# Three PSUM banks in one ring for the maxima products and the projections of the masked attention layers

## The chip, the cores and the metric

The kernel runs on one core of a Trainium2 chip. A time is the device time of one execution in microseconds (us). The parts of a core are called PE (TensorE, the matmul engine, with PEld for its weight loads), DVE (VectorE), ACT (ScalarE), POOL (GpSimd) and SP (SyncE, which here only issues DMAs). PE writes its results to PSUM, a memory of eight banks of 128 x 512 fp32 values; DVE and ACT read them from there. The engines run independently and meet at semaphores.

## The reference, cut to what matters

The network has four layers of attention and feed-forward over `x` of shape (8, 512, 256). Layers 0, 1 and 3 have attention under a mask; layer 2 (relative positions) and the four feed-forward parts are not touched by the change.

```python
# layer 1 (layers 0 and 3 alike, without adj and with a finite value for masked scores)
Q, K, V = heads(layernorm(x), Wq), heads(ctx, Wk), heads(ctx, Wv)   # 16 heads of 16
scores  = einsum('bhqd,bhkd->bhqk', Q, K) / sqrt(16) + adj
scores  = where(mask == 0, -inf, scores)
out     = einsum('bhqk,bhkd->bhqd', softmax(scores, axis=-1), V)
x       = x + out.transpose(0, 2, 1, 3).reshape(b, s, 256) @ Wo.T + bo
```

## The kernel before, in words

`masked_attention` does one masked layer. A layer is a row of frames, one for each of the 8 batches (b from -1, which only prepares, to 8, which only finishes). A frame has 16 steps s and each step two positions, p = 2s and p = 2s + 1; every engine walks through the same 32 positions in an order written out by hand, and they differ only in what they wait for.

The row maxima come first, in a product of their own, seven steps ahead of their use. In position p PE makes two of them, which this text calls p1(2p) and p1(2p+1) (line 261, one 96-row bf16 matmul of 128 x 512 each). DVE adds the mask and takes the maximum (line 460), and the semaphore `maxed` says that it has read the bank. The two banks `p1_ps0` and `p1_ps1` alternate, so p1(u) waits until p1(u-2) has been read.

In the same position PE makes the scores of two heads, transposed, into `p2_ps` (line 276). In even positions ACT has put the mask there before (the "seed", line 512); in odd positions of layers 0 and 3 PE adds it with two more matmuls (line 281). In layer 1 ACT seeds both. ACT takes the exponential (line 529). At the end of each odd position PE multiplies the probabilities of the step before by V (line 292, eight instructions).

Between these stand the shared units, which all use the one bank `front_ps`: the transposes of the normalized input (xT, line 223), the projections k, q (line 230), v (line 235) and out (line 242), and the turned maxima m (line 251). A unit of the first five kinds has two pieces. In PE's order of an even position it is: p1(2p), scores, piece 0, p1(2p+1), piece 1. The units stand at positions 0 (v0), 4 (v1), 8 (out0), 12 (out1), 14 and 16 (xT0, xT1), 20 and 22 (k0, k1), 24 and 28 (q0, q1); m stands at 3, 11, 19 and 27, behind the scores of an odd position, and also waits for `m_split`, the last of four small DVE instructions (line 414) that stand between and behind the maxima of the position before. A unit of position p is read in position p + 1: xT, k, q and m by ACT, which in position p + 1 comes to it before that position's exponential but behind the exponential and the seed of position p; v and out by DVE, before the maxima of position p + 1. The semaphore `front_read` counts these reads, and each unit waits for the one before it.

A layer starts with eight units in a row, `FIRST` (xT0, xT1, k0, k1, q0, q1, v0, v1), all through `front_ps`. DVE splits the two k and the two q results into three bf16 parts each (lines 430 to 436), SP stacks them by twelve DMAs (line 613) into `k_stack` and `q_stack`, and the first p1 waits for both stacks. SP gives out these DMAs behind loads of masks, which wait for POOL. At the end of a layer out0 and out1 follow each other.

## Time and profile before

| | us |
|---|---|
| median of 3 runs | 3845.13 (3836.37 to 3846.18) |
| the profiled execution | 3849.17 |
| its span, first to last instruction | 3847.4 |
| PE busy | 3198.5 (83%) |
| DVE busy | 2500.1 (65%) |
| ACT busy | 2215.1 (58%) |
| POOL busy | 1118.4 (29%) |
| p1 matmuls (line 261), 1536 of them | 603.0, idle before them 119.2 |
| maxima (line 460), 1536 of them | 1038.7, idle before them 434.5 |
| exponentials (line 529), 768 of them | 781.3, idle before them 275.4 |

The masked layers run from 16 to 671 us (layer 0), from 975 to 1702 us (layer 1) and from 2782 to 3437 us (layer 3). Shares over the whole span mix them with the other stages, so a masked layer has to be read from its own stretch. "Idle before" is time in which the engine did nothing ahead of an instruction of the group; the name behind the arrow is what it waited for. A matmul's time in the trace reaches from its start to the end of its result, and consecutive matmuls overlap, so the distance between two starts says more than the duration: two p1 next to each other start 0.22 us apart if nothing holds them. A row of busy time by stretch (rows 1) gives the stretch, its length, then for PE, PEld, DVE, ACT and POOL the busy time and the number of instructions, then the granted clock of TensorE as a share of 2.4 GHz, the busy share of the DMA engines and GB/s.

### The profile page before, as it was taken

The numbers are of one execution on the slowest core, as the hardware profiler recorded it, in microseconds if no ns is written. First come the engines' busy times: TensorE is split into PE (matmuls) and PEld (weight loads), VectorE is DVE, ScalarE is ACT, GpSimd is POOL, SyncE is SP. The second block draws the span as 40 slices with busy tenths as digits, with TensorE's granted clock in tenths as the row PEclk, the third lists the DMA queues.
The fourth block names the chain that finished last, engine by engine and source line by source line (L and its number), as shares of the span: only waits on it lengthen the run. The fifth ranks groups of instructions, "written<-read, shape, count | busy, mean of one in ns | idle before, by whom it ended". The sixth has DMA issues, their size and how long they took to land. (4 is left out here: it accounts for less than half of the span.)

```text
span 3847.4 us, 67593 instructions
## 1 busy us (share of the span) xinstructions
PE 3198.5 (83%) x17361; PEld 1628.5 (42%) x17361; DVE 2500.1 (65%) x7668; ACT 2215.1 (58%) x2970; POOL 1118.4 (29%) x1194
## 2 busy tenths in 40 slices
PE   5999998899588888858987888888379999965997
PEld 3343332344333333225654555555134334325565
DVE  4777775777677677744225777878867777755431
ACT  1777777444188888962115666667537777750111
POOL 4344440000545555401104333321232211101332
PEclk8999999899799899988998999999589999985899
DMA  5322420000433333310018998997031221102232
GB/s 146 87 70 73 101 62 12 22 1 1 130 105 89 89 94 89 83 52 0 0 39 277 293 292 288 308 310 267 19 87 40 56 63 40 35 25 97 74 101 66
DMA packets 212153, 392.86 MB, mean 102 GB/s; under 512 B 24633, under 2 KB 76985, under 8 KB 211657
## 3 DMA queue, kind: packets, MB, share of 16 engines
q1 hardware_dynamic: 168777, 296.38, 27.8%
q10 hardware_dynamic: 36864, 83.90, 5.8%
q0 software_dynamic: 6144, 8.39, 1.3%
q8 instruction: 143, 2.34, 0.3%
q14 instruction: 225, 1.84, 0.2%
HBM read 189.88 MB, written 96.47 MB: 74 GB/s over the span
## 5 line engine op out<-in xcount | busy, mean ns | idle before, releaser
L460 DVE CUSTOM_DVE_ANT_0 A_sums<-A_p_ps,A_bias 128x512 bf16<-128x512 f32 x1536 | 1038.7, 687 | 434.5 <-PE A_p_ps L261 397.1
L529 ACT ACTIVATE A_probs<-A_p_ps 128x1024 f32<-128x1024 f32 x768 | 781.3, 1018 | 275.4 <-PE A_p_ps L276 184.9
L261 PE MATMUL A_p_ps<-A_k_stack,A_q_stack 96*128 96x512 bf16 x1536 | 603.0, 395 | 119.2 <-DVE A_nmax L460 110.3
L512 ACT ACTIVATE A_p_ps<-A_biasT 128x1024 f32<-128x1024 bf16 (+1 forms) x512 | 526.1, 1028 | 62.3 <-ACT A_probs L529 2.8
L276 PE MATMUL A_p_ps<-A_q_stack,A_k_stack 99*128 99x512 bf16 x1536 | 468.1, 386 | 41.3 <-ACT A_p_ps L512 36.6
L292 PE MATMUL A_oT_ps<-A_probs,A_v_aug 128*17 128x512 f32 x3072 | 417.5, 616 | 0.7 <-ACT A_probs L529 0.7
L261 PEld LDWEIGHTS A_p_ps<-A_k_stack,A_q_stack 96*128 96x128 bf16 x1536 | 149.4, 97 | 634.3 <-DVE A_nmax L460 541.5
L1100 DVE CUSTOM_DVE_ANT_0 A_scores<-A_qk_ps,A_rel_in 128x384 f32<-128x384 f32 (+3 forms) x512 | 232.4, 486 | 83.2 <-PE A_qk_ps L984 75.3
L1007 PE MATMUL A_t_ps<-ident,A_scores 128*128 128x128 f32 x1280 | 228.8, 301 | 58.2 <-DVE A_probsT L1090 49.9
L1090 DVE COPY A_probsT<-A_t_ps 128x384 f32<-128x384 f32 (+3 forms) x512 | 229.4, 485 | 55.7 <-PE A_t_ps L1007 48.2
L1155 ACT ACTIVATE A_rel_out<-A_rel_ps 128x1024 f32<-128x1024 f32 (+3 forms) x256 | 180.2, 704 | 144.8 <-PE A_rel_ps L973 143.5
L1162 ACT ACTIVATE A_scores<-A_scores,A_nmax 128x384 f32<-128x384 f32 (+3 forms) x512 | 257.5, 555 | 7.6 <-DVE A_nmax L1100 7.4
L276 PEld LDWEIGHTS A_p_ps<-A_q_stack,A_k_stack 99*128 99x128 bf16 x1536 | 143.4, 99 | 179.4 <-ACT A_p_ps L512 73.2
L1182 POOL TENSOR_SCALAR_AFFINE_SELECT A_rel_in<-A_rel_in 128x256 f32<-128x256 f32 x256 | 103.4, 412 | 396.3 <-DMA A_rel_in<-A_rel_dram 390.5
L1007 PEld LDWEIGHTS A_t_ps<-ident,A_scores 128*128 128x128 f32 x1280 | 152.3, 149 | 135.5 <-DVE A_probsT L1090 57.0
L574 POOL TENSOR_SCALAR A_bias<-A_mask_in 128x512 bf16<-128x512 int32 (+2 forms) x68 | 132.0, 1941 | 207.6 <-DVE A_nmax L460 187.5
L1517 PE MATMUL B_cv_ps<-B_hs,B_tap_diag 128*128 128x512 f32 x384 | 180.6, 607 | 2.6 <-DVE B_hs L1619 2.4
L574 POOL TENSOR_SCALAR A_biasT<-A_mask_in 128x512 bf16<-128x512 int32 (+2 forms) x68 | 131.8, 1938 | 138.8 <-PE A_p_ps L281 70.2
L2773 ACT ACTIVATE M_hid<-M_h_ps,M_b 128x512 f32<-128x512 f32 x64 | 44.0, 688 | 189.3 <-PE M_h_ps L2575 185.7
L281 PE MATMUL A_p_ps<-A_biasT,ident_bf 128*128 128x512 bf16 x512 | 152.5, 378 | 0.0
L555 POOL CAST A_parts<-A_qk 128x512 bf16<-128x512 f32 x84 | 51.3, 611 | 336.1 <-ACT A_qk L497 335.6
L2092 ACT ACTIVATE U_hid<-U_h_ps,U_hid_bias 128x512 f32<-128x512 f32 x64 | 44.0, 687 | 177.5 <-PE U_h_ps L1930 177.5
(343 smaller groups left out, 5436.4 us busy)
## 6 DMA issues: line engine op xcount, KB each, us to landing
A_k_stack<-A_parts SPq DMA_DIRECT2D x192, 256.0 KB, 5.0
A_q_stack<-A_parts SPq DMA_DIRECT2D x192, 256.0 KB, 5.5
A_rel_dram<-A_rel_out ACTq DMA_DIRECT2D x64, 512.0 KB, 4.9
A_rel_in<-A_rel_dram SPq DMA_DIRECT2D x64, 512.0 KB, 5.3
A_rel_dram<-A_rel_out ACTq DMA_DIRECT2D x64, 384.0 KB, 4.8
A_rel_in<-A_rel_dram SPq DMA_DIRECT2D x64, 384.0 KB, 5.1
A_ctxT<-in_ctxT SPq DMA_DIRECT2D x32, 512.0 KB, 6.5
A_mask_in<-in_mask SPq DMA_DIRECT2D x64, 256.0 KB, 4.7
```

Source lines behind the costliest of these rows:

```text
L261: nc.tensor.matmul(p1_ps[i % 2][:, :], q_stack[0:KS, a_par, j * GH + i, t * P:(t + 1) * P], k_stack[0:KS, a_par, j * GH + i, :], start=Tru ...
L276: last = nc.tensor.matmul(p2_ps[half][:, i % 2, :], k_stack[:, par, j * GH + i, kb * P:(kb + 1) * P], q_stack[:, par, j * GH + i, :], star ...
L292: nc.tensor.matmul(oT_ps[CW * i:CW * i + HD + 1, :], v_aug[:, v_par, kb, j * GH + i, :], probs[:, (s - 1) % 2 * 2 + i // 2, i % 2, :], sta ...
L460: nc.vector.tensor_tensor_reduce(out=sums[:, i % NX, :], in0=p1_ps[i % 2][:, :], in1=bias[:, t, :], scale=-1.0, scalar=3.4028235e38, op0=A ...
L512: nc.scalar.activation(p2_ps[half][:, :, :], turned, ACT.Copy).then_inc(seeded, 1)
L529: nc.scalar.activation(probs[:, s % 2 * 2 + half, :, :], p2_ps[half][:, :, :], ACT.Exp).then_inc(exp_done, 1)
L574: last = nc.gpsimd.tensor_scalar(dst, mask_in[:, k % 2, :], 0.0, NEG, ALU.is_equal, ALU.mult)
L1007: last = nc.tensor.transpose(t_ps[:, i, kb, :], scores[(p - TURN_LAG) % NP][:, i, kb * P:(kb + 1) * P], ident[:, :])
L1090: nc.vector.tensor_copy(probsT[u % NP][:, i, 0:nk, :], t_ps[:, i, 0:nk, :]).then_inc(copied, 1)
L1100: nc.vector.tensor_tensor_reduce(out=scores[p % NP][:, i, 0:n], in0=qk_ps[i][:, 0:n], in1=rel_in[s % NI][:, (2 * half + i) * n:(2 * half + ...
L1162: nc.scalar.activation(scores[u % NP][:, i, 0:n], scores[u % NP][:, i, 0:n], ACT.Exp, bias=nmax[:, u % NP, i:i + 1], scale=-1.0).then_inc( ...
L1517: last = nc.tensor.matmul(cv_ps[c % 2][:, :], tap_diag[:, c, k, :], hs[:, c % 2, k:k + S], start=k == 0, stop=k == 2)
```

## The change

`p1_ps0`, `p1_ps1` and `front_ps` become `ring_ps0` to `ring_ps2`. The turns of a frame are listed in PE's order, `p1(2p)`, the shared unit of position p if there is one, `p1(2p+1)`; each takes the next of the three banks. There are 78 turns in a frame, 26 times three, so a turn has the same bank in every frame. A turn waits until the turn three before it has been read. `front_read` is split into `act_read` and `dve_read`, as two engines' counts can no longer be one count. The number and the order of the instructions on PE, DVE, ACT, POOL and SP stay; what changes is which semaphore and value a turn waits for, and which bank it uses.

```diff
-        p1_ps = [pb(f"p1_ps{i}", [P, S], F32) for i in range(2)]
+        ring_ps = [pb(f"ring_ps{i}", [P, S], F32) for i in range(RING)]
...
-        front_ps = pb("front_ps", [P, S], F32)
...
-        front_read = sem("front_read")
+        act_read, dve_read = sem("act_read"), sem("dve_read")
...
+        def ring_turns():
+
+            turns = []
+            for p in range(HALVES):
+                turns.append(("p1", 2 * p))
+                turns += [(k, i) for _, k, i in shared(PLAN, p)]
+                turns.append(("p1", 2 * p + 1))
+            return turns
...
+        def wait_for_bank(pe, b, kind, i):
+
+            at = TURNS.index((kind, i))
+            same = [u for n, u in enumerate(TURNS) if n % RING == at % RING]
+            here = same.index((kind, i))
+            for back, turns in ((0, same[:here]), (1, same)):
+                for k, n in reversed(turns):
+                    if in_ring(b - back, k, n):
+                        if k == "p1":
+                            pe.wait_ge(maxed, ((b - back) * STEPS + LEAD) * GH + n + 1)
+                        else:
+                            pe.wait_ge(dve_read if k in ("v", "out") else act_read, read_of(b - back, k, n))
+                        return
...
         def pe_max_unit(pe, b, a, a_par, i):
-            unit = (b * STEPS + a) * GH + i
             _, _, j, t = ahead(a - LEAD)
-            if later(unit - 1):
-                pe.wait_ge(maxed, unit - 1)
-            nc.tensor.matmul(p1_ps[i % 2][:, :], q_stack[0:KS, a_par, j * GH + i, t * P:(t + 1) * P],
+            turn = ("p1", (a - LEAD) * GH + i)
+            wait_for_bank(pe, b, *turn)
+            nc.tensor.matmul(bank(*turn)[:, :], q_stack[0:KS, a_par, j * GH + i, t * P:(t + 1) * P],
                              k_stack[0:KS, a_par, j * GH + i, :], start=True, stop=True).then_inc(p1_done, 1)
...
-                for n, kind, i in here:
-                    pe_shared(pe, n, kind, i, uses_before(b), b, 0)
                 for n, kind, i in shared(plan, p):
                     if kind == "m":
-                        pe_maxima(pe, n, i, uses_before(b), b)
+                        pe_maxima(pe, i, b)
+                    else:
+                        wait_for_bank(pe, b, kind, i)
+                        pe_shared(pe, bank(kind, i), kind, i, b, 0)
...
+                if n >= RING:
+                    pe.wait_ge(dve_read if FIRST[n - RING][0] == "v" else act_read, first_read(n - RING))
                 for piece in range(2):
-                    pe_shared(pe, n, kind, i, 0, -2, piece)
+                    pe_shared(pe, ring_ps[n % RING], kind, i, -2, piece)
```

On PE, in positions 14 and 15 of a steady frame of layer 0 (xT0 and the position behind it; `A0_qk32` is the normalized input, `ISA` an instruction that computes a wait's value or waits), before the change:

```order
L223 MATMUL A0_front_ps<-ident,A0_qk32 128x128
L260 ISA
L261 MATMUL A0_p1_ps1<-A0_k_stack,A0_q_stack 128x512 [waits A0_maxed]
L223 MATMUL A0_front_ps<-ident,A0_qk32 128x128 x2
L260 ISA
L261 MATMUL A0_p1_ps0<-A0_k_stack,A0_q_stack 128x512 [waits A0_maxed]
L274 ISA
L276 MATMUL A0_p2_ps1<-A0_q_stack,A0_k_stack 128x512 [waits A0_exp_done]
L276 MATMUL A0_p2_ps1<-A0_q_stack,A0_k_stack 128x512
L281 MATMUL A0_p2_ps1<-A0_biasT,ident_bf 128x512 x2
L260 ISA
L261 MATMUL A0_p1_ps1<-A0_k_stack,A0_q_stack 128x512 [waits A0_maxed]
```

and with the change, in the same place:

```order
L282 MATMUL A0_ring_ps2<-ident,A0_qk32 128x128
L237 ISA
L322 MATMUL A0_ring_ps0<-A0_k_stack,A0_q_stack 128x512 [waits A0_maxed]
L282 MATMUL A0_ring_ps2<-ident,A0_qk32 128x128 x2
L237 ISA
L322 MATMUL A0_ring_ps1<-A0_k_stack,A0_q_stack 128x512 [waits A0_maxed]
L335 ISA
L337 MATMUL A0_p2_ps1<-A0_q_stack,A0_k_stack 128x512 [waits A0_exp_done]
L337 MATMUL A0_p2_ps1<-A0_q_stack,A0_k_stack 128x512
L342 MATMUL A0_p2_ps1<-A0_biasT,ident_bf 128x512 x2
L239 ISA
L322 MATMUL A0_ring_ps2<-A0_k_stack,A0_q_stack 128x512 [waits A0_act_read]
```

Nothing moved, but the last of these, p1(31), now uses the bank of xT0 and waits for ACT's read of it, where it waited for a maximum before. The same holds at the second p1 behind every shared unit of an even position; behind v and out the wait is for `dve_read`.

On PE, in the first shared units of layer 0, before and with the change:

```order
L223 MATMUL A0_front_ps<-ident,A0_qk32 128x128 [waits A0_xn_ready]
L223 MATMUL A0_front_ps<-ident,A0_qk32 128x128 x3
L223 MATMUL A0_front_ps<-ident,A0_qk32 128x128 [waits A0_front_read]
L223 MATMUL A0_front_ps<-ident,A0_qk32 128x128 x3
L230 MATMUL A0_front_ps<-A0_ctxT,A0_wk 128x256 [waits built,A0_front_read,zeroed]
L230 MATMUL A0_front_ps<-A0_ctxT,A0_wk 128x256 x3
L230 MATMUL A0_front_ps<-A0_ctxT,A0_wk 128x256 [waits A0_front_read]
L230 MATMUL A0_front_ps<-A0_ctxT,A0_wk 128x256 x3
```

```order
L282 MATMUL A0_ring_ps0<-ident,A0_qk32 128x128 [waits A0_xn_ready]
L282 MATMUL A0_ring_ps0<-ident,A0_qk32 128x128 x3
L282 MATMUL A0_ring_ps1<-ident,A0_qk32 128x128 x4
L291 MATMUL A0_ring_ps2<-A0_ctxT,A0_wk 128x256 [waits built,zeroed]
L291 MATMUL A0_ring_ps2<-A0_ctxT,A0_wk 128x256 x3
L291 MATMUL A0_ring_ps0<-A0_ctxT,A0_wk 128x256 [waits A0_act_read]
L291 MATMUL A0_ring_ps0<-A0_ctxT,A0_wk 128x256 x3
```

xT1 no longer waits for the read of xT0, and likewise k0 and k1 run up to three units ahead of their reads.

## Rows read from the trace of the kernel before

**Rows 1.** Busy time by stretch: steady part of layer 0, of layer 1.

```profile
170.00:640.00 470.00, 441.03 (x2367) 179.97 (x2364) 363.90 (x1115) 357.00 (x393) 181.10 (x143) 1.00 0.28 70
1080.00:1640.00 560.00, 471.15 (x2311) 182.87 (x2309) 406.25 (x1218) 487.64 (x533) 282.65 (x224) 0.93 0.33 91
```

**Rows 2.** Groups by line: the p1 matmuls, busy, mean ns, idle before.

```profile
L261 PE MATMUL A_p_ps<-A_k_stack,A_q_stack 96*128 96x512 bf16 x1536 | 603.0, 395 | 119.2 <-DVE A_nmax L460 110.3 <-issue 4.9 <-DMA A_q_stack<-A_parts 1.8
```

**Rows 3.** Timeline (start, us, instruction), layer 0: end of maximum 12, p1(14).

```profile
324.66 0.08 DVE L460 DVE_READ_ACCUMULATOR2_ANT A_nmax<- 128x1 f32 x1
...
324.80 0.39 PE L261 MATMUL A_p_ps<-A_k_stack,A_q_stack 96*128 96x512 bf16 x1 [0.30 <-DVE A_nmax L460]
```

**Rows 4.** Timeline, layer 0: p1(31), the read of xT0, scores of position 16.

```profile
345.37 0.38 PE L261 MATMUL A_p_ps<-A_k_stack,A_q_stack 96*128 96x512 bf16 x1
...
345.99 0.58 ACT L484 ACTIVATE A_xnT<-A_front_ps 128x512 f32<-128x512 f32 x1
...
346.89 0.60 PE L276 MATMUL A_p_ps<-A_q_stack,A_k_stack 99*128 99x512 bf16 x2
```

**Rows 5.** Timeline, layer 0, the read of k0 and p1(43).

```profile
357.86 0.67 ACT L497 ACTIVATE A_qk<-A_front_ps,A_bk 128x512 f32<-128x512 f32 x1
...
358.50 0.38 PE L261 MATMUL A_p_ps<-A_k_stack,A_q_stack 96*128 96x512 bf16 x1
```

**Rows 6.** Timeline, layer 0: reads of v1 and out1, with p1(11) and p1(27).

```profile
321.81 0.72 DVE L374 TENSOR_TENSOR A_v_aug<-A_front_ps,A_bv_bc 128x256 f32<-128x256 f32 x2
322.17 0.38 PE L261 MATMUL A_p_ps<-A_k_stack,A_q_stack 96*128 96x512 bf16 x1
...
341.29 0.65 DVE L394 TENSOR_TENSOR x_sb<-A_front_ps,x_sb 128x512 f32 x1
341.64 0.38 PE L261 MATMUL A_p_ps<-A_k_stack,A_q_stack 96*128 96x512 bf16 x1
```

**Rows 7.** Timeline, layer 0: p1(38), the last split, m.

```profile
351.99 0.39 PE L261 MATMUL A_p_ps<-A_k_stack,A_q_stack 96*128 96x512 bf16 x1 [0.56 <-DVE A_nmax L460]
...
352.76 0.18 DVE L414 TENSOR_TENSOR A_m_parts<-A_m_rest,A_m_parts 128x16 bf16<-128x16 f32 x1
353.18 0.39 PE L251 MATMUL A_front_ps<-ident_bf,A_m_parts 128*12 128x128 bf16 x4
```

**Rows 8.** Timeline of ACT, layer 1: read of xT0, exponential of position 16.

```profile
1250.00 0.58 ACT L484 ACTIVATE A_xnT<-A_front_ps 128x512 f32<-128x512 f32 x1
...
1252.57 1.01 ACT L529 ACTIVATE A_probs<-A_p_ps 128x1024 f32<-128x1024 f32 x1
```

**Rows 9.** Timeline, layer 1: read of out1, exponential of position 14.

```profile
1245.36 0.88 DVE L389 SCALAR_TENSOR_TENSOR x_sb<-A_front_ps,A_nan_rows,x_sb 128x256 f32 x2 [0.21 <-issue]
...
1247.89 1.02 ACT L529 ACTIVATE A_probs<-A_p_ps 128x1024 f32<-128x1024 f32 x1 [0.44 <-PE A_p_ps L276]
```

**Rows 10.** Timeline, layer 1: p1(51), the read of q0, m behind it.

```profile
1274.42 0.38 PE L261 MATMUL A_p_ps<-A_k_stack,A_q_stack 96*128 96x512 bf16 x1
...
1274.74 0.67 ACT L497 ACTIVATE A_qk<-A_front_ps,A_bq 128x512 f32<-128x512 f32 x1
...
1280.23 0.59 PE L251 MATMUL A_front_ps<-ident_bf,A_m_parts 128*12 128x128 bf16 x4 [2.09 <-DVE A_m_parts L414]
```

**Rows 11.** Timeline, starts of layers 3 and 1: xT1, k0, k1; stack DMA; first p1.

```profile
2790.47 1.11 PE L223 MATMUL A_front_ps<-ident,A_qk 128*128 128x128 f32 x4 [0.69 <-ACT A_xnT L484]
2792.31 3.75 PE L230 MATMUL A_front_ps<-A_ctxT,A_wk 128*128 128x256 f32 x8 [0.73 <-issue]
2796.91 3.78 PE L230 MATMUL A_front_ps<-A_ctxT,A_wk 128*128 128x256 f32 x8 [0.84 <-ACT A_qk L497]
...
2804.09 3.94 SPq L613 DMA_DIRECT2D A_k_stack<-A_parts  x6
...
1018.35 1.04 PE L261 MATMUL A_p_ps<-A_k_stack,A_q_stack 96*128 96x512 bf16 x2 [1.81 <-DMA A_q_stack<-A_parts]
```

**Rows 12.** Timeline, end of layer 0: out1.

```profile
666.59 3.78 PE L242 MATMUL A_front_ps<-A_wo,A_heads_outT 128*128 128x256 f32 x8 [0.90 <-DVE x_sb L394]
```

More of the change, by code:

```diff
@@ L185, in use_of, with reads_before, count @@
             return uses_before(b) + [u[1:] for u in (plan_of(b) if isinstance(b, int) else PLAN)].index((kind, i))
+        def reads_before(b, kind):
+            alike = [k for k in ("xT", "k", "q", "m", "v", "out") if (k in ("v", "out")) == (kind in ("v", "out"))]
+            def count(units):
+                return sum(u[-2] in alike for u in units)
+            if not isinstance(b, int):
+                return count(PLAN) * b + (reads_before(1, kind) - count(PLAN))
+            return count(FIRST) + sum(count(plan_of(i)) for i in range(-1, b))
@@ new lines, in read_of, with first_read @@
+        def read_of(b, kind, i):
+            units = [u[1:] for u in (plan_of(b) if isinstance(b, int) else PLAN)]
+            alike = [u for u in units if (u[0] in ("v", "out")) == (kind in ("v", "out"))]
+            return reads_before(b, kind) + alike.index((kind, i)) + 1
+        def first_read(n):
+            kinds = [(k == "v") for k, _ in FIRST]
+            return kinds[:n + 1].count(kinds[n])
+        def ring_turns():
[5 more added lines that the diff above has]
+            return turns
@@ new lines, in in_ring, with bank @@
+        def in_ring(b, kind, i):
+            if kind == "p1":
+                return has(b, i // 4 + LEAD)
+            return not isinstance(b, int) or (kind, i) in [u[1:] for u in plan_of(b)]
+        def bank(kind, i):
+            return ring_ps[TURNS.index((kind, i)) % RING]
+        def wait_for_bank(pe, b, kind, i):
[10 more added lines that the diff above has]
+                        return
+                if isinstance(b, int) and b - back < 0:
+                    n = [n for n in range(len(FIRST)) if n % RING == at % RING][-1]
+                    pe.wait_ge(dve_read if FIRST[n][0] == "v" else act_read, first_read(n))
+                    return
@@ L211, in seeds, with pe_shared @@
             return b * sum(by_act(*u) for u in HALVES_OF) + sum(by_act(*u) for u in HALVES_OF[:s * 2 + half + 1])
-        def pe_shared(pe, n, kind, i, base, b, piece):
-            if piece == 0 and later(base + n):
-                pe.wait_ge(front_read, base + n)
+        def pe_shared(pe, front_ps, kind, i, b, piece):
             cols = slice(piece * D, (piece + 1) * D)
@@ L227, in pe_shared @@
                     pe.wait_ge(ctx_in, (b + 3) * 16)
+                if kind == "q" and i == 0 and piece == 0:
+                    pe.wait_ge(act_read, read_of(b, "xT", 1) if later(b + 2) else first_read(1))
                 wt, src = (wq_sb, xnT) if kind == "q" else (wk_sb, ctxT)
@@ L245, in pe_shared, with pe_maxima @@
                 last.then_inc(front_full, 1)
-        def pe_maxima(pe, n, j, base, b):
-            pe.wait_ge(front_read, base + n)
+        def pe_maxima(pe, j, b):
+            front_ps = bank("m", j)
+            wait_for_bank(pe, b, "m", j)
             pe.wait_ge(m_split, b * NG + j + 1)
@@ L317, in pe_positions @@
                 for n, kind, i in here:
-                    pe_shared(pe, n, kind, i, uses_before(b), b, 1)
+                    pe_shared(pe, bank(kind, i), kind, i, b, 1)
                 if half == 1 and has(b, s - 1):
@@ L377, in dve_shared @@
                         bv_bc[:, :].rearrange("p (h d) -> p h d", d=HD), ALU.add)
-                last.then_inc(front_read, 1)
+                last.then_inc(dve_read, 1)
             else:
@@ L390, in dve_shared @@
                                                               nan_rows[:, 1 - par, t:t + 1], tile, ALU.add, ALU.add)
-                    last.then_inc(front_read, 1)
+                    last.then_inc(dve_read, 1)
                     return
@@ L460, in dve_positions @@
                         nc.vector.tensor_tensor_reduce(
-                            out=sums[:, i % NX, :], in0=p1_ps[i % 2][:, :], in1=bias[:, t, :],
+                            out=sums[:, i % NX, :], in0=bank("p1", s * GH + i)[:, :], in1=bias[:, t, :],
                             scale=-1.0, scalar=3.4028235e38, op0=ALU.add, op1=ALU.min,
```

29 lines of the change are left out of this document (15 added, 14 removed).

## The prediction

> **What bounds the kernel now.** I read the busy time of the masked layers' steady stretches first. In layer 0 PE is busy for 441.0 of 470 us at a granted clock of 1.00 (2.4 GHz), ACT 357.0, DVE 363.9 [rows 1]: PE bounds it, and layer 3 is built alike. In layer 1, where ACT also writes the mask for both halves, ACT leads with 487.6 of 560 us and PE has 471.2 [rows 1]. Next the groups by line: the p1 matmuls had 119.2 us of idle time before them, 110.3 of it until DVE had read the bank [rows 2]. That is what a third bank could give back, 37 us a layer. Then I read the timeline of one frame position by position, because the change gives the third bank by taking it from the shared units. Two questions decide: where does a p1 wait now that need not, and what will the new waits for the shared units' reads cost?
>
> **Part 1, p1 with no shared unit near.** Where p1(2p+2) directly follows p1(2p+1) it waits for the maximum of p1(2p) of the same step. p1(14) started 0.06 behind the end of maximum 12 (324.74) and 0.30 of idle time stand before it [rows 3]; with the 0.16 by which a p1's 0.38 outlasts its 0.22 of distance, that is a stall of 0.46. The ring frees this place. Only six steps of a frame have no unit in their even position, and four of these have an m in the odd one. The two clean ones are positions 7 and 31. At 31 I take the whole 0.46, at 7 only 0.3, since DVE works through the statistics of the input behind it. In a layer: 7 x 0.46 + 8 x 0.3 = 5.6 us.
>
> **Part 2, the four steps with m.** There p1(38) shows the same stall, 0.56 idle, 0.72 with the tail [rows 7]. But behind it in PE's order stands m, and m needs the last split, which ended at 352.94, while m started at 353.18 [rows 7]. The splits hang on the maxima of p1(36) and p1(37), not on p1(38). So the stall moves from p1(38) to m: at most 353.18 - 353.00 = 0.18 is left of the 0.72. Bounds 0 and 0.72; I take 0.1, nearest to this row. 4 x 7 x 0.1 = 2.8 us a layer.
>
> **Part 3, the new waits.** Behind a unit of an even position p, three turns on, stands p1(2p+3). It used to wait for a maximum long past and now waits for the unit's read, with V's product and the next scores queued behind it on PE. What this costs is the end of the read, plus 0.06, minus the start that p1 had. In layer 0:
> - xT: ACT reads it only behind an exponential and a seed. The read ended at 345.99 + 0.58 = 346.57, p1(31) started at 345.37 [rows 4]: 1.26 us. The transposes are short, so PE is there early. Twice in a frame: 2.52. ACT waits for PE's scores in the next step, so nothing hides it.
> - k and q: 357.86 + 0.67 + 0.06 against 358.50 [rows 5]: 0.09, four times: 0.36.
> - v1, read by DVE: 322.59 against 322.17 [rows 6]: 0.42; v0, for which no row stands here, 0.04.
> - out1: 342.00 against 341.64 [rows 6]: 0.36. out0 stands where DVE is late anyway and the next p1 waits for it: 0.
>
> xT, k and q come in six frames with scores, v and out in seven: 6 x 2.88 + 7 x 0.46 + 7 x 0.36 = 23.0 us. The same rows in frames 1 to 5 repeat these values within a few hundredths. Net of parts 1 and 2: 23.0 - 8.4 = 14.6 us in layer 0, the same in layer 3. If ACT were the bound behind xT, the 15.1 us of the two xT would vanish; if a wait also made the next one later, they could grow by a half. These are the bounds: -0.5 and 22 for each layer.
>
> **Part 4, layer 1.** ACT works without a gap over long parts here. From the end of a read (1250.58) to the exponential of the next position but one, ACT has work for 1.99 us (1252.57) [rows 8]. PE, let go by this read, needs 0.06 and then the 2.12 us from p1(31) at 345.37 to the end of the scores at 347.49 [rows 4]. That is 0.2 too late even if ACT starts at once; I take 0.3. It applies to xT0, k0, k1 and q1; behind xT1 and q0 ACT has another copy to do that covers it. 1.2 us a frame. q0 costs through PE: the read ended at 1275.41, p1(51) had started at 1274.42 [rows 10], 1.05 us, and on the next p1 hangs the split for which m waited 2.09 us [rows 10]. I take 0.9. out1: its read ended at 1246.24; with 0.06 and 2.12 the scores end at 1248.42, and the exponential had started at 1247.89 after 0.44 of idle time [rows 9]: 0.6. v0, v1 and out0 fall where DVE's splits or ACT's copy of m set the pace: 0. Sum: 6 x 2.1 + 7 x 0.6 = 16.8; the clean steps, half hidden by ACT, give back 1.5: 15.3 us. Bounds 4 (only where ACT idles) and 26 (v and out0 too).
>
> **Part 5, ends of a layer.** At its start xT1, k0 and k1 waited 0.69, 0.73 and 0.84 for a bank [rows 11] and no longer do, so k's parts are ready some 2.3 to 2.8 us earlier, and the stacks' DMAs, which leave as soon as they are (2804.09) [rows 11], start the first p1. I take 3.0 in layers 0 and 3, as later waits of the row of eight go too (bounds 1 and 5.5), and 0 in layer 1, where p1 waited for the DMA of q_stack, 1.81 us [rows 11], and the stacks stood behind loads of masks on SP. Frame -1, where DVE often waits for PE, gives 0.7 a layer (0 to 2); out1 at the end no longer waits for DVE's read of out0, 0.90 [rows 12]. 6.0 + 2.1 + 2.7 = 10.8 us.
>
> **Sum.** 14.6 + 14.6 + 15.3 - 10.8 = 33.7 us. On the profiled execution (3849.2, span 3847.4 and 1.8 around it) that makes 3882.9. It lies 4.0 above the median of the runs, 3845.1, so for a median I expect 3879.
>
> A rule against this result: the Trainium skill, page "Perfetto Trace Analysis", section "Identifying Performance Opportunities", says that a gap repeating on the engine that should be saturated can mean that there is not enough PSUM for the next tile. The trace has that repeating gap. By the rule the ring would pay; what the rule does not see is that the bank comes from another user.
>
> **Rivals.**
> - *The gaps go for good* (faster). Place: the four m steps. If the splits ended earlier once PE is ahead, m would not take over the stall, and (0.72 - 0.1) x 4 x 7 x 3 = 52 us come back: 3827. It decides from the point at which the split ends more than 0.18 before m; in rows 7 it ends 0.24 before, 0.18 of it usable, and DVE's work in between does not depend on p1(38). Chance 0.07.
> - *ACT's wait is hidden* (no change). If PE's pause at xT in layers 0 and 3 falls into time that PE would lose later, 30.2 us go: 3849. For it: ACT has 357 of 470 us and PE often stands at a semaphore. Against it: PE is busy for 94% [rows 1]. Chance 0.10.
> - *The clock falls* (much slower). Layer 1, with more gaps, was granted 0.93 where layer 0 got 1.00 [rows 1]. If layers 0 and 3 fell to that, PE's 441 us in 470 would grow by 7%, 31 us in such a stretch and 62 for both layers: 3941. The gaps that come are of 1.26 us, twice in a frame of 16 steps. Chance 0.05. The Trainium skill ("TensorE: Matmul & The Clock Gate", section "A second HAM failure mode: psum-queue depth-cycling") describes a kernel that cycles PSUM banks and loses throughput as its clock swings; no row here shows that for layer 0.
> - *It does not do what it says*: waits equal to the old ones where units stand, and reads that land sooner than I think, with ends and clean steps about even. 3845. Chance 0.04.
>
> **How the numbers follow.** The forecast has 0.74, with its own range 3858 to 3900: layers 0 and 3 from 8 to 22 each, layer 1 from 8 to 22, ends from 5 to 18, not all at one end together. Over 0.3% (11.5 us, about what a measurement of this kernel can tell from no change) slower is above 3856.7. Faster 0.07; the same 0.10 + 0.04, less a little for the upper half of the hidden case, 0.13; slower the rest, 0.80. The range for 8 in 10 takes in the hidden case and leaves out the clock: 3848 to 3902.
>
> **What would show it.** In the profile after, the p1 group must have less idle time until DVE's maxima, but new idle time until ACT's copy of xT (about 30 us over layers 0 and 3) and of q and k, and until DVE's reads of v and out. m must show more idle time until the last split than before. In the rows at xT0, p1(31) must start 0.06 behind the end of ACT's read. The frames of layer 0 must be some 2.4 us longer, and the first p1 of layers 0 and 3 must come some 3 us earlier from the layer's start, in layer 1 not. I am wrong if m starts earlier against p1(36), if the frame gets shorter, or if the granted clock of layer 0 leaves 1.00.

## The result, and the profile after

| | before | after |
|---|---|---|
| median (4 runs each) | 3845.26 us | 3879.72 us |
| lowest to highest | 3836.37 to 3846.18 | 3873.70 to 3880.74 |
| the profiled execution, span | 3849.17, 3847.4 | 3880.62, 3878.9 |

The ratio is 1.0092 with a 95% interval of [1.0078, 1.0107]. The forecast was 3879 us. The terms behind it did not all come out as written, and one pair of them cancelled, so the layers are read one by one. The table is worked out from the two timelines, one execution of each kernel: the length of each masked layer from DVE's leaving the barrier ahead of it to the barrier behind it, cut at the first maxima of the frames (us).

| after minus before | layer 0 | layer 1 | layer 3 | sum | forecast |
|---|---|---|---|---|---|
| start to the first maximum | -2.7 | -0.3 | -4.2 | -7.2 | -6.0 |
| frame -1 | -2.9 | +0.1 | +0.5 | -2.3 | -2.1 |
| seven frames | +16.6 | +13.8 | +14.6 | +45.0 | +44.5 |
| last frame to the end | -3.1 | +2.3 | -2.2 | -3.0 | -2.7 |
| layer | +8.0 | +15.8 | +8.7 | +32.5 | +33.7 |

The other stages took 1.0 us less, by the difference of the spans (31.5). How much of such a difference is the change can be seen from the kernel `ends` below, whose seven frames are as before the change: they are 4.3, 3.5 and -0.5 us longer there in layers 0, 1 and 3. So a term of 2 or 3 us in one cell says little. In layers 0 and 3 frames 1, 4 and 5 repeat to 0.01 us between those two kernels; in them the change costs 2.70 us a frame in layer 0 and 2.77 in layer 3, where the terms of the prediction make 2.54.

First the groups by line, as [rows 2]: the p1 matmuls and m after. The row of m before, which did not stand ahead of the prediction, comes behind them.

```profile
L322 PE MATMUL A_ring_ps<-A_k_stack,A_q_stack 96*128 96x512 bf16 x1536 | 579.3, 395 | 135.9 <-ACT A_xnT L546 43.5 <-DVE A_nmax L522 30.0 <-DMA A_q_stack<-A_parts 17.8
L313 PE MATMUL A_ring_ps<-ident_bf,A_m_parts 128*12 128x128 bf16 x384 | 38.5, 225 | 89.2 <-DVE A_m_parts L476 89.1
```

```profile
L251 PE MATMUL A_front_ps<-ident_bf,A_m_parts 128*12 128x128 bf16 x384 | 39.2, 228 | 35.2 <-DVE A_m_parts L414 35.0
```

The main moves stand in these rows. p1's wait for the maxima went from 110.3 to 30.0 us, so the third bank did what a third bank does. Of these 80 us, 54 came back at m, whose wait for the split rose from 35.0 to 89.1, and 43.5 us are a wait for ACT's copy of xT that was not there before. 17.8 us are waits for the DMAs that stack q at the start of the three layers (5.5, 9.2 and 3.1): p1 now comes to them earlier. They cost nothing, since the first p1 of each layer is not later for it but 0.3 to 4.2 us earlier.

The timeline of layer 0 after, at xT0 (ACT's read of it, p1(31)), to be held against [rows 4]:

```profile
349.88 0.58 ACT L546 ACTIVATE A_xnT<-A_ring_ps 128x512 f32<-128x512 f32 x1
...
350.51 0.39 PE L322 MATMUL A_ring_ps<-A_k_stack,A_q_stack 96*128 96x512 bf16 x1 [1.09 <-ACT A_xnT L546]
```

p1(31) starts 0.05 behind the end of the read (349.88 + 0.58); in [rows 4] it started 1.20 ahead of that end. And at the m of the step behind it, to be held against [rows 7]: the end of maximum 37, the last split, m, p1(39).

```profile
358.97 0.08 DVE L522 DVE_READ_ACCUMULATOR2_ANT A_nmax<- 128x1 f32 x1
...
359.18 0.19 DVE L476 TENSOR_TENSOR A_m_parts<-A_m_rest,A_m_parts 128x16 bf16<-128x16 f32 x1
359.42 0.39 PE L313 MATMUL A_ring_ps<-ident_bf,A_m_parts 128*12 128x128 bf16 x4 [0.49 <-DVE A_m_parts L476]
...
359.74 0.39 PE L322 MATMUL A_ring_ps<-A_k_stack,A_q_stack 96*128 96x512 bf16 x1
```

p1(38) had no idle time left before it, and m has 0.49.

To see all turns at once I took the distance from the start of each p1 to the start of the p1 before it, as a mean over frames 1 to 5 of layer 0. Turns that are not in the table changed by less than 0.06 us.

| place | before | after | difference |
|---|---|---|---|
| p1(14), p1(62): clean steps | 0.68, 0.68 | 0.22, 0.22 | -0.92 |
| p1(6), (22), (38), (54) | 0.80, 1.41, 0.90, 0.80 | 0.22 each | -3.03 |
| p1(7), (23), (39), (55), behind m | 2.10, 1.57, 1.52, 1.51 | 2.65, 2.66, 2.06, 1.93 | +2.61 |
| p1(31), p1(35): xT | 1.10, 1.09 | 2.35, 2.35 | +2.50 |
| p1(43), (47), (51), (59): k, q | 1.09 each | 1.17 each | +0.34 |
| p1(11): v1 | 1.09 | 1.51 | +0.43 |
| p1(27): out1 | 1.09 | 1.45 | +0.36 |
| p1(17), p1(19): out0 | 1.78, 1.10 | 1.94, 1.21 | +0.27 |
| p1(8) | 1.31 | 1.52 | +0.21 |

p1(8) shows the same 0.21 in xt_alone and kq_alone below, where nothing near it was changed, so I do not put it down to the ring. Frames 1 to 5 of layer 0 are 2.94 us longer by this (77.58 against 74.64), those of layer 3 2.63.

Last the busy time by stretch, as [rows 1], for layer 0 and layer 1 after:

```profile
170.00:640.00 470.00, 429.04 (x2256) 178.12 (x2289) 353.26 (x1083) 346.24 (x381) 180.87 (x143) 1.00 0.28 69
1089.00:1649.00 560.00, 451.55 (x2243) 177.40 (x2242) 393.28 (x1186) 475.18 (x517) 281.35 (x223) 0.95 0.33 91
```

Layer 0 kept its granted clock of 1.00 with PE busy for 12 us less in the 470. (That is not all idle time: the frames are longer, so the stretch holds fewer matmuls, and of layer 0 as of layer 3 the trace after lacks 46 records of matmuls.) Layer 1 rose from 0.93 to 0.95, which I had not expected. A part of it lies at k0. These are stretches of 2 us there in frame 1, of before and of after:

```profile
1178.00:1180.00 2.00, 0.45 (x2) 0.43 (x3) 0.00 (x0) 1.61 (x3) 0.00 (x0) 1.00 0.00 0
1180.00:1182.00 2.00, 2.00 (x7) 1.36 (x6) 0.19 (x1) 1.85 (x2) 0.00 (x0) 0.50 0.01 3
1182.00:1184.00 2.00, 2.00 (x8) 1.00 (x6) 1.29 (x4) 0.52 (x1) 0.00 (x0) 0.64 0.20 28
```

```profile
1191.00:1193.00 2.00, 1.05 (x5) 0.64 (x4) 0.70 (x2) 1.61 (x3) 0.00 (x0) 1.00 0.00 0
1193.00:1195.00 2.00, 2.00 (x11) 1.19 (x9) 1.15 (x3) 1.88 (x3) 0.00 (x0) 1.00 0.01 4
```

Before, the clock was granted at 0.50 (1.2 GHz) for these 2 us and partly for the next, after a stretch in which PE was busy for 0.45 of 2 us; after, PE was busy for 1.05 of 2 us there and the clock stayed at 1.00. The first of the two rows of k0's matmuls is of before, the second of after:

```profile
1179.55 1.64 PE L230 MATMUL A_front_ps<-A_ctxT,A_wk 128*128 128x256 f32 x4 [2.08 <-ACT A_m_row L490]
```

```profile
1192.32 1.13 PE L291 MATMUL A_ring_ps<-A_ctxT,A_wk 128*128 128x256 f32 x4 [0.94 <-ACT A_m_row L552]
```

ACT leads in layer 1, and k0 waits for ACT's read of m. PE was held up at xT before it came here, so it waits 0.94 where it waited 2.08, and then works at full speed. From p1(40) to p1(42) frames 1, 3 and 5 need 2.7 to 3.0 us less than before.

The long wait at k0 is not all there is to the clock, though. Frames 2 and 4 of before have a fall of the clock too, but ahead of k0: V's product between p1(39) and p1(40) runs at 0.50, the wait at k0 is only 0.8 to 0.9, and the clock is back at 1.00 when k0 starts. V's product in frame 4, then in frame 1, both of before:

```profile
1429.05 1.83 PE L292 MATMUL A_oT_ps<-A_probs,A_v_aug 128*17 128x512 f32 x8
```

```profile
1175.47 1.05 PE L292 MATMUL A_oT_ps<-A_probs,A_v_aug 128*17 128x512 f32 x8
```

After, the clock stays at 1.00 from p1(38) to p1(43) in frames 0 to 5, and frames 2 and 4 need 0.5 us less from p1(40) to p1(42) and 0.8 less ahead of p1(40).

### The profile page after: what moved, and what is told of

Read it like the earlier page. It is cut to its first block and busy times, and to the rows that moved or that the text cites. A ratio compares the mean times of both kernels' runs of the same rounds, so it can differ in the third digit from the quotient of the medians.

```text
span 3878.9 us, 67500 instructions
## 1 busy us (share of the span) xinstructions
PE 3170.0 (82%) x17253; PEld 1624.1 (42%) x17361; DVE 2498.8 (64%) x7668; ACT 2218.0 (57%) x2970; POOL 1117.0 (29%) x1194
## 5 line engine op out<-in xcount | busy, mean ns | idle before, releaser
L522 DVE CUSTOM_DVE_ANT_0 A_sums<-A_ring_ps,A_bias 128x512 bf16<-128x512 f32 x1536 | 1043.9, 688 | 494.6 <-PE A_ring_ps L322 453.8
L322 PE MATMUL A_ring_ps<-A_k_stack,A_q_stack 96*128 96x512 bf16 x1536 | 579.3, 395 | 135.9 <-ACT A_xnT L546 43.5
L574 ACT ACTIVATE A_p_ps<-A_biasT 128x1024 f32<-128x1024 bf16 (+1 forms) x512 | 526.1, 1028 | 62.4 <-ACT A_probs L591 2.8
L322 PEld LDWEIGHTS A_ring_ps<-A_k_stack,A_q_stack 96*128 96x128 bf16 x1536 | 148.3, 98 | 655.3 <-DVE A_nmax L522 364.9
L1047 PE MATMUL A_qk_ps<-A_k_stack,A_q_stack 96*128 96x384 bf16 (+3 forms) x512 | 126.5, 312 | 12.8 <-DVE A_nmax L1163 11.1
```

Of the source, the lines that this page charges most:

```text
L322: nc.tensor.matmul(bank(*turn)[:, :], q_stack[0:KS, a_par, j * GH + i, t * P:(t + 1) * P], k_stack[0:KS, a_par, j * GH + i, :], start=True ...
L522: nc.vector.tensor_tensor_reduce(out=sums[:, i % NX, :], in0=bank("p1", s * GH + i)[:, :], in1=bias[:, t, :], scale=-1.0, scalar=3.4028235 ...
L574: nc.scalar.activation(p2_ps[half][:, :, :], turned, ACT.Copy).then_inc(seeded, 1)
```

## The experiments

All are compared with the kernel before on the same chip. I write "ends" for the first kernel, since most of the others stand on it. Lengths of the masked layers come from the profiled execution (before: 656.6, 727.8, 654.9; after: 664.5, 743.6, 663.6). The last column is the mean length of frames 1, 4 and 5 in layers 0 and 3, the ones that repeat, less that of the kernel before (after: +2.70, +2.77).

| kernel | median | ratio, 95% interval | layers 0, 1, 3 | a frame, layers 0, 3 |
|---|---|---|---|---|
| ends | 3836.1 | 0.9978 [0.9969, 0.9987] | 652.3, 729.5, 648.1 | 0.00, 0.00 |
| xt_alone | 3864.2 | 1.0061 [1.0041, 1.0080] | 670.3, 727.2, 661.9 | +2.55, +2.46 |
| kq_alone | 3852.0 | 1.0023 [1.0008, 1.0038] | 656.5, 734.7, 648.8 | +0.39, +0.32 |
| vout_alone | 3852.8 | 1.0023 [1.0014, 1.0033] | 660.3, 733.7, 652.7 | +0.96, +1.06 |
| all_waits | 3893.3 | 1.0128 [1.0111, 1.0146] | 680.3, 741.8, 670.7 | +3.84, +3.93 |
| borrow | 3817.7 | 0.9930 [0.9914, 0.9947] | 644.0, 727.8, 641.9 | -0.96, -0.71 |
| ring_early | 3843.0 | 1.0001 [0.9991, 1.0012] | 649.6, 738.2, 644.3 | +0.36, +0.42 |
| ring_mfree | 3837.9 | 0.9988 [0.9977, 1.0000] | 649.2, 726.3, 649.9 | +1.19, +1.24 |
| before_mfree | 3826.8 | 0.9945 [0.9924, 0.9965] | 658.4, 728.7, 653.9 | -0.40, -0.48 |
| ends_mlate | 3822.0 | 0.9964 [0.9941, 0.9987] | 655.5, 715.1, 648.1 | -0.09, -0.25 |
| ring_late_early | 3821.3 | 0.9949 [0.9933, 0.9966] | 641.8, 730.5, 634.2 | -0.46, -0.62 |
| best | 3799.5 | 0.9893 [0.9868, 0.9919] | 639.6, 721.8, 633.9 | -1.32, -1.28 |

The layers' lengths come from one execution of each kernel, and not always from a typical one: the profiled execution lies 22.8 us above the median in before_mfree, 7.2 in all_waits and 6.4 in vout_alone, and 6.9 below it in kq_alone, 4.0 in ring_mfree and 3.0 in ends. What is said below of layer 1, which has no frames that repeat so well, is therefore held against the ratios too.

**ends: the start alone.** The ring's rule (a turn waits for the last user of its bank) works with any table of banks, so I gave it one that repeats the old assignment and left the ring only in the row of eight. In `bank_table` (not shown) the first argument lists positions whose p1 borrows the units' bank, the second the positions of units whose bank passes to the second p1 behind them:

```diff
         def bank(kind, i):
 
-            return ring_ps[TURNS.index((kind, i)) % RING]
+            return ring_ps[BANKS[TURNS.index((kind, i))]]
...
-            same = [u for n, u in enumerate(TURNS) if n % RING == at % RING]
+            same = [u for n, u in enumerate(TURNS) if BANKS[n] == BANKS[at]]
...
+        BANKS = bank_table((), ())     # shared units: bank 2; p1: banks 0 and 1 in turn
```

> The three banks as before the change in every frame (shared units in one bank, p1 in two), and only the eight units at the start of a layer take the three in turn. My theory: what the change gives at the start is 2.7 us in layer 0, 4.2 in layer 3, 0.3 in layer 1, as the two traces show, so 3845 - 7 = 3838 us, ratio 0.998. Rival: the earlier start is given back, since the frames behind it wait for masks or for DMAs anyway: 3845, ratio 1.000.

Measured 3836.1, 0.9978: the start's part is real and lasts. The start is the same in the changed kernel, and in the profile after the start of layer 3 shows why (DVE's first instruction, xT0 and xT1, k0 and k1, the first stack DMA), to be held against [rows 11]:

```profile
2805.60 0.48 DVE L814 MEMSET A_oT_ps<- 128x512 f32 x1 [1.23 <-PEq L37]
2811.21 1.97 PE L282 MATMUL A_ring_ps<-ident,A_qk 128*128 128x128 f32 x8 [9.54 <-DVE A_qk L400]
...
2812.97 5.65 PE L291 MATMUL A_ring_ps<-A_ctxT,A_wk 128*128 128x256 f32 x16
...
2823.28 3.90 SPq L674 DMA_DIRECT2D A_k_stack<-A_parts  x6
```

The idle times of 0.69, 0.73 and 0.84 are gone, and the first stack DMA leaves 17.68 us behind DVE's first instruction. Before it left 21.03 behind it, worked out from this row of before and the 2804.09 of [rows 11]:

```profile
2783.06 0.48 DVE L751 MEMSET A_oT_ps<- 128x512 f32 x1 [1.23 <-PEq L37]
```

**xt_alone, kq_alone, vout_alone: one kind of wait each.** The table gives the second p1 behind the named units the bank of that unit; all else as in ends.

```diff
-        BANKS = bank_table((), ())
+        BANKS = bank_table((), (14, 16))            # xt_alone: p1(31), p1(35)
+        BANKS = bank_table((), (20, 22, 24, 28))    # kq_alone: p1(43), (47), (51), (59)
+        BANKS = bank_table((), (0, 4, 8, 12))       # vout_alone: p1(3), (11), (19), (27)
```

> As the kernel with only the start changed, but p1(31) and p1(35) take the bank of xT0 and xT1, and so wait for ACT's read of them; all other turns keep the old banks. My theory (the wait for xT costs 1.26 us each, nothing hides it): 12 x 1.26 = 15.1 us in layer 0 and as much in layer 3, and in layer 1, where the trace after shows it given back in every second frame, 4 to 12 us: 3838 + 30 + 8 = 3876 us, ratio 1.008. Rival (ACT's wait is hidden, and the slowdown comes from the other waits): within 5 us of 3838, ratio 0.998.

> As the kernel with only the start changed (3836), but the second p1 behind k0, k1, q0 and q1 takes the bank of that unit and waits for ACT's read of it; all other turns keep the old banks. My theory, by the terms of the prediction: 6 x 4 x 0.09 = 2.2 us in each of layers 0 and 3 (measured on the trace after: 0.34 a frame), and in layer 1, where ACT has no time left, 6 x (0.9 + 0.9) = 10.8 without xT0's part 9.0: 3836 + 4.4 + 9.0 = 3849 us, ratio 1.001. Rival (layer 1's cost comes from elsewhere, as for xT, whose wait cost nothing there): 3840, ratio 0.999.

> As the kernel with only the start changed (3836), but the second p1 behind v0, v1, out0 and out1 takes the bank of that unit and waits for DVE's read of it; all other turns keep the old banks. My theory, by the terms of the prediction: 7 x (0.46 + 0.36) = 5.7 us in each of layers 0 and 3, and in layer 1 7 x 0.6 = 4.2 for out1: 3836 + 15.6 = 3852 us, ratio 1.002. Rival (in layer 1 the four waits, of 0.5 to 1.1 us each on the trace after, are not covered by ACT): 7 x 2.5 = 17 us there, 3865, ratio 1.005.

In layers 0 and 3 the sum of xt_alone is 31.9 us over ends, against 30.2 expected (frames 1 to 5 of layer 0: p1(31) and p1(35) 1.25 later each). With the start alone the same kernel was below before, with xT's waits added it is clearly above, so ACT's wait is not hidden there. vout_alone has 12.6 us over ends in the two layers, against 11.4, and 1.0 a frame against 0.82, since out0 is not free. kq_alone has 0.3 to 0.4 a frame, against 0.36. (Its layers, 4.2 and 0.7 us over ends, make 4.9 against 4.4, but by luck: 3.5 of the 4.2 lie outside the seven frames.)

In layer 1 the profiled executions give less than the terms of the prediction for two of the three. kq_alone costs 5.1 us there against 10.8 (the 9.0 in the expectation is a slip of mine: three times 0.3 and 0.9 make 1.8 a frame). vout_alone costs 4.2, as forecast, but as with kq_alone less than 1 us of it lies in the seven frames, the rest in frame -1 and at the end. xT costs nothing: -2.3. The ratios bear this out only in part. kq_alone is 0.45% slower than ends, some 17 us, and layers 0 and 3 account for 4 of it, so its layer 1 may well cost the 10.8; the profiled execution was a fast one. xt_alone is 0.83% slower, some 32 us, of which layers 0 and 3 account for 30. Little is left for layer 1 there. Both of these rests are uncertain by 7 or 8 us. In the profile, xT's two waits are there in full (p1(31) +1.45, p1(35) +1.04 in frames 1 to 5, against before), but 1.2 of them go at p1(39) and p1(40), the two p1 behind m, and 1.9 at p1(41) and p1(42), by the shorter wait at k0 and by the clock. The granted clock of its steady stretch was 0.95, as in the changed kernel:

```profile
1082.00:1642.00 560.00, 465.26 (x2321) 179.26 (x2321) 409.71 (x1232) 490.02 (x536) 285.18 (x225) 0.95 0.34 92
```

**all_waits: the ten waits at once**, `bank_table((), (0, 4, 8, 12, 14, 16, 20, 22, 24, 28))`.

> As the kernel with only the start changed (3836), with all ten waits for a unit's read (xT, k, q, v, out) at once, and without the freed p1 of the clean steps and the steps with m. My theory: the prediction's part 3, 23.0 us in each of layers 0 and 3; in layer 1 the sum of the three kernels with one kind of wait each, measured at -2.3, +5.1 and +4.2 there, 7 us: 3836 + 46 + 7 = 3889 us, ratio 1.012. Rival for layer 1 (the waits do not add up: what one is covered by is gone with the next): 14 us or more there, 3896 or more, ratio 1.014.

Measured 3893.3, between the two. Layer 3 has 22.6 us over ends, where part 3 said 23.0; layer 0 has 28.1, of which 3.4 lie in frame -1. Layer 1 has 12.3, where the single kinds make 7.0, but one profiled execution of each does not settle whether they add up. A frame of layers 0 and 3 is 3.8 to 3.9 us longer, by 0.1 to 0.2 more than the 3.70 of part 3, which left out0 at 0.

**borrow: the third bank only where no unit needs it.** p1(14) and p1(62) take the units' bank; in the steps with m at positions 19 and 27, p1(38) and p1(54) take it, and m gets the bank of p1(36) or p1(52), which is then the units' bank.

```diff
-        BANKS = bank_table((), ())
+        BANKS = bank_table((7, 19, 27, 31), ())
```

> As the kernel with only the start changed, but p1(14) and p1(62), and p1(38) and p1(54) in the steps with m, take the bank of the shared units, where no unit needs it. No p1 waits for a unit's read here. My theory: p1(14) and p1(62) start 0.46 us earlier, the steps with m at positions 19 and 27 give 0.15 each as the stall moves to m: 1.2 us a frame, 9 us in each of layers 0 and 3, 0 to 6 in layer 1: 3838 - 21 = 3817 us, ratio 0.993. Rival 1 (the gaps at the steps with m go for good): 0.6 more for each of the two in a frame, 26 us more, 3791, ratio 0.986. Rival 2 (a p1 that starts earlier brings nothing, since ACT or DVE sets the pace): 3838, ratio 0.998.

Measured 3817.7, 0.9930, as the theory had it. The groups of p1 and m in ends, and then in borrow:

```profile
L344 PE MATMUL A_ring_ps<-A_k_stack,A_q_stack 96*128 96x512 bf16 x1536 | 603.4, 395 | 131.3 <-DVE A_nmax L544 109.9 <-DMA A_q_stack<-A_parts 13.5 <-issue 5.9
L335 PE MATMUL A_ring_ps<-ident_bf,A_m_parts 128*12 128x128 bf16 x384 | 39.0, 227 | 34.7 <-DVE A_m_parts L498 34.5
```

```profile
L344 PE MATMUL A_ring_ps<-A_k_stack,A_q_stack 96*128 96x512 bf16 x1536 | 584.7, 393 | 95.2 <-DVE A_nmax L544 75.7 <-DMA A_q_stack<-A_parts 14.8 <-issue 2.6
L335 PE MATMUL A_ring_ps<-ident_bf,A_m_parts 128*12 128x128 bf16 x384 | 38.6, 225 | 52.4 <-DVE A_m_parts L498 52.3
```

p1 waits 34.2 us less for the maxima, and m 17.8 more for the split: two of the four borrowed turns pass their stall on, two keep the gain. Layers 0 and 3 are 14.4 us shorter than in ends and layer 1 is 1.8 shorter, without a single wait for a unit's read. This kernel and the changed one differ only in who uses the third bank when, and they lie 1.6% apart.

**ring_early: the same ring, xT read a seed earlier.**

```diff
                 for n, kind, i in shared(plan, p, 1):
-                    act_shared(act, n, bank(kind, i), kind, i, uses_before(b), b, par)
+                    if kind != "xT":
+                        act_shared(act, n, bank(kind, i), kind, i, uses_before(b), b, par)
...
+                for n, kind, i in shared(plan, p):      # behind the exponential of position p
+                    if kind == "xT":
+                        act_shared(act, n, bank(kind, i), kind, i, uses_before(b), b, par)
                 if has(b, s + 1) and by_act(t, half):
                     act_seed(act, b, over, t, half)
```

> The changed kernel, but ACT reads xT in the position of the unit itself, behind the exponential and before the seed, so about 1.02 us earlier (a seed's time). My theory: p1 behind it starts 1.02 us earlier, 12 times in each of layers 0 and 3: 24.5 us, and 0 to 10 us in layer 1: 3880 - 29 = 3851 us, ratio 1.0015. Rival (the wait for xT covers time that would be lost later anyway): under 5 us gained, 3876 or more, ratio 1.008.

Measured 3843.0: the ring's whole loss against before is gone by the order of two instructions on ACT. (Against ends, which has the better start too, 0.2% is left.) At xT0 in layer 0:

```profile
340.72 0.59 ACT L546 ACTIVATE A_xnT<-A_ring_ps 128x512 f32<-128x512 f32 x1
341.20 1.04 ACT L574 ACTIVATE A_p_ps<-A_biasT 128x1024 f32<-128x1024 bf16 x1
341.37 0.39 PE L322 MATMUL A_ring_ps<-A_k_stack,A_q_stack 96*128 96x512 bf16 x1
```

The read stands ahead of the seed (L574), and p1(31) has no idle time. Its distance to the p1 before it fell from 2.35 to 1.18, so 1.17 a turn instead of 1.02, and the layers became shorter by 15.0, 5.4 and 19.3 us against the ring.

**ring_mfree and before_mfree: m without the split.** m multiplies a tile of zeros written once, in the ring and in the kernel before. Both leave out the true maxima: the scores get zeros in their place.

```diff
-            pe.wait_ge(m_split, b * NG + j + 1)
             for t in range(TPB):
                 last = nc.tensor.matmul(front_ps[0:GH * 3, t * P:(t + 1) * P],
-                                        m_parts[:, t, :, :].rearrange("p h k -> p (h k)"), ident_bf[:, :],
+                                        m_fixed[:, :], ident_bf[:, :],
```

> The changed kernel, but m multiplies a tile of zeros that is written once, so that PE does not wait for the split of the maxima (the maxima that reach the exponential are zero). My theory (p1(38)'s stall went to m because m needs the last split): p1(39) then waits only for maximum 37, which ended 0.6 to 0.7 us before p1(39) started: 4 x 0.63 a frame, 18 us in each of layers 0 and 3, 0 to 15 in layer 1: 3880 - 44 = 3836 us, ratio 0.998; layer 0's frames 75.0 us. Rival (m's stall is not the split, or what it gives back is lost at the next maxima): over 3865, ratio above 1.005.

> The kernel before, with m on the tile of zeros in the same way. My theory: here p1(38) still waits for maximum 36, and m started only 0.18 us behind the end of the scores: 4 x 0.18 a frame, 5 us in each of layers 0 and 3, 0 to 10 in layer 1: 3844 - 15 = 3829 us, ratio 0.996. So the distance between the ring and before falls from 36 to about 7 us. Rival (the stalls of the steps with m have nothing to do with the split): both kernels lose the same, and the distance stays 30 to 36 us.

The ring gained 41.8 us by it, the kernel before 15.5, by the medians; the distance between them fell from 34.5 to 11.1 (the five runs of before_mfree spread over 35 us, and by the ratios 16 or 17 are left). That is the theory's side, though not all of the 0.63 stayed: in frames 1, 4 and 5 of layers 0 and 3 the ring got back 1.5 us a frame, not 2.5, and the kernel before 0.4, not 0.7. Layer 0 of ring_mfree, behind p1(38):

```profile
351.11 0.39 PE L313 MATMUL A_ring_ps<-ident_bf,A_m_fixed 128*12 128x128 bf16 x4
...
351.21 0.08 DVE L522 DVE_READ_ACCUMULATOR2_ANT A_nmax<- 128x1 f32 x1
...
351.43 0.39 PE L322 MATMUL A_ring_ps<-A_k_stack,A_q_stack 96*128 96x512 bf16 x1
...
353.01 0.57 ACT L552 ACTIVATE A_m_row<-A_ring_ps 12x512 bf16<-12x512 f32 x1
...
353.72 1.13 PE L292 MATMUL A_ring_ps<-A_ctxT,A_wk 128*128 128x256 f32 x4 [0.17 <-ACT A_m_row L552]
```

m starts at once, but k0 then waits for ACT's read of m, and p1(41) behind it comes 0.41 later. The frames 1 to 5 of layer 0 took 75.9 us, not 75.0.

**ends_mlate, best, ring_late_early: m behind V's product.** If m is the one that waits, nothing should stand behind it.

```diff
-                for n, kind, i in shared(plan, p):
-                    if kind == "m":
-                        pe_maxima(pe, i, b)
...
                 if half == 1 and has(b, s - 1):
                     pe_values(pe, b, s, par)
+                for n, kind, i in shared(plan, p):
+                    if kind == "m":
+                        pe_maxima(pe, i, b)
```

ends_mlate is ends with this edit; ring_late_early is ring_early with it. best is borrow with it, and with out1 of the last frame in bank 1:

```diff
+        def bank_in(b, kind, i):
+            return ring_ps[1] if last_out(b, kind, i) else bank(kind, i)
...
+            if last_out(b, kind, i):
+                pe.wait_ge(maxed, B * STEPS * GH)
+                return
```

> The kernel with only the start changed, with the old banks, but PE makes m behind V's product instead of ahead of the second p1 of its step. My theory: m's wait for the split, 0.18 us in layers 0 and 3, is covered by that p1 and V's product: 4 x 0.18 a frame, 5 us in each, and in layer 1, where m waits for up to 2 us, 10 us: 3836 - 20 = 3816 us, ratio 0.993. Rival (ACT reads m later, so the units that wait for this read come later): 3836 or more, ratio 0.998.

> The kernel in which p1(14), p1(62), p1(38) and p1(54) take the units' bank (3818), with m behind V's product, and with out1 of the last frame in a bank of its own. My theory: behind p1(38) and p1(54) m no longer holds PE until the split, 0.6 us each, at the other two steps with m 0.18 each, 1.5 us a frame, 11 in each of layers 0 and 3, 10 in layer 1, 1 to 3 at the end of a layer: 3818 - 36 = 3782 us, ratio 0.984. Rival (the next p1 or the next unit waits instead, for the maxima of the step or for ACT's read of m, as p1(41) did by 0.41 when m waited for nothing): half of it, 3800, ratio 0.989.

> The ring of the change, with ACT's read of xT ahead of the seed (3843) and m behind V's product. My theory: the stall that p1(38) and its like passed on to m is now covered at all four steps, 0.55 each, 16 us in each of layers 0 and 3, 10 in layer 1: 3843 - 42 = 3801 us, ratio 0.989. Rival, as before: half of it, 3822, ratio 0.995. Against the kernel that only borrows the bank it would still lose by the waits for v, out, k and q, 16 us and more.

ends_mlate gained 14 us over ends by the medians, but only 0.14%, some 5 us, by the ratios, whose intervals overlap; its ten runs spread from 3811.6 to 3849.0. So a gain is not shown. In the profile it lies in layer 1 (715.1 against 729.5); in layers 0 and 3 there was next to nothing to cover (0.1 to 0.25 a frame), where I expected 5 us each. In best and in ring_late_early the rival's numbers came out, nearly to the microsecond: 3799.5 and 3821.3, half of what I hoped for. For best that was partly luck, since it has two edits. Of its 18 us below borrow, 5.6 lie behind the first maximum of the last frame in layers 0 and 3, where out1 has its own bank; a frame is only 0.4 to 0.6 us shorter than in borrow, where I expected 1.5. ring_late_early has 0.8 to 1.0 a frame below ring_early, where I expected 2.2. The place, in layer 0 of best: p1(39), V's product, m, ACT's read of m, k0, p1(41).

```profile
345.20 0.39 PE L355 MATMUL A_ring_ps<-A_k_stack,A_q_stack 96*128 96x512 bf16 x1 [0.18 <-DVE A_nmax L555]
...
345.52 1.05 PE L386 MATMUL A_oT_ps<-A_probs,A_v_aug 128*17 128x512 f32 x8
...
346.39 0.39 PE L346 MATMUL A_ring_ps<-ident_bf,A_m_parts 128*12 128x128 bf16 x4
...
347.11 0.57 ACT L585 ACTIVATE A_m_row<-A_ring_ps 12x512 bf16<-12x512 f32 x1
...
347.82 1.13 PE L324 MATMUL A_ring_ps<-A_ctxT,A_wk 128*128 128x256 f32 x4 [0.29 <-ACT A_m_row L585]
...
348.78 0.38 PE L355 MATMUL A_ring_ps<-A_k_stack,A_q_stack 96*128 96x512 bf16 x1
```

m waits for nothing any more, but k0 uses m's bank, and p1(41), 0.57 further from its predecessor than before, hands the gap on. Even so, best is the fastest, 1.1% below the kernel before and 2% below the change.

## Why the prediction was right, and where it was not

- **What bounds it.** Right. PE bounds layers 0 and 3: waits of PE that were added there by themselves (xt_alone, kq_alone, vout_alone, all_waits) came out in the frames at their full size, and what borrow took away net of m's wait showed in them too.
- **Part 1, clean steps.** Right in kind, small in size: 0.46 at p1(14) too, where I took 0.3 for fear of DVE's other work. 0.92 a frame, not 0.76.
- **Part 2, m.** Right. 3.03 us a frame less before p1(38) and its like, 2.61 more behind m: 0.42 is left, where four times 0.1 were forecast. ring_mfree shows that it is the split: without it the ring wins 42 us, where the kernel before wins 15 to 21.
- **Part 3, the new waits.** xT 2.50 a frame against 2.52, k and q 0.34 against 0.36, v1 0.43 against 0.42, out1 0.36 against 0.36. The term that failed is out0, put at 0: p1(17) and p1(19) are 0.27 later. all_waits gives the sum: 22.6 us in layer 3, 28.1 in layer 0, where frame -1 and the ends scatter, against 23.0.
- **Part 4, layer 1.** The size of the layer was right (+15.8 against 13.7 with its ends), the working behind it was not. "xT0, k0, k1 and q1 0.3 each" and "v0, v1 and out0 0" are too small: on the trace after, the second p1 behind each of the ten units is 0.4 to 1.5 us later, xT1 and v0, v1, out0 among them. Against that stands a step that was missing altogether: PE's wait at k0 gets shorter by a part of what was lost ahead of it, and a fall of the granted clock to 0.50 near k0 goes away in every frame. xt_alone shows both halves in its profile, +2.5 a frame at xT and nothing for the layer, and the fall is gone in all its six frames, where ends has it in all six. Two errors of opposite sign met, so that the sum came out right here was luck.
- **Part 5, ends.** Start -7.2 against -6.0, with 4.2 in layer 3 alone, and 0.3 in layer 1 against 0; the kernel ends confirms it. Frame -1 in sum right, but all of it in layer 0. At the end of a layer -3.1 and -2.2, but +2.3 in layer 1. These last two terms are not shown to come from the change: ends, where the banks of these frames are the old ones, has -2.3, -1.0 and -0.9 in frame -1, and -3.6, 0.0 and -0.4 at the end, against before.
- **The rivals.** The gaps go for good: no, m starts 0.05 us behind the end of the split, and there alone 54 us are given back. ACT's wait is hidden: wrong for layers 0 and 3, by xt_alone; true for xT in layer 1, as far as its profile and the ratios tell. The clock falls: layer 0 stayed at 1.00, and layer 1 rose.

The rule of the Trainium skill that I weighed the result against is confirmed in its first half only. The same page, "Perfetto Trace Analysis", section "Matmuls", also says: "Independent matmul groups should rotate through different PSUM banks so the ACT/DVE evacuation of one overlaps the next group's matmuls". The changed kernel rotates more evenly than the one before and is 0.9% slower; the rotation of borrow is uneven and 0.7% faster, 0.2% of that by the start. So on this kernel the even rotation lost by the banks in it that were emptied late, and ring_early, which empties them earlier behind xT, costs nothing against the kernel before.

## What to carry to other kernels

A ring makes every turn wait for the reader of the turn a fixed number ahead of it, so users whose results are read late (behind an exponential and a seed) should not share a ring with users that are read at once; give the extra bank away by a table, only at the turns where its own user is idle. When a wait on the bounding engine is removed, look at the next instruction in that engine's order and at what it needs: if that comes later than the stall you removed, the gain moves there, and here it did so twice, from p1 to m and from m to k0. Before buying a bank, try to read the slow one earlier: one swap on ACT was worth as much as the whole ring cost. (Whether the swap would also help the kernel before, where no p1 waits for xT, was not tried.)
